# Edge loads at a round's second landing, x1 stored without a hold at B's end, five z rounds fetched there

## The chip, the cores and the metric

The kernel runs on one core of a Trainium2 chip. The metric is the device time of one execution in microseconds; lower is better. All tensors are fp32.

## The reference

Two layers of a graph network over 50000 nodes of 128 features, with 25000 edges sorted by target `dst`:

```python
h = relu(layernorm(x))
agg = segment_sum(h[src], dst) / max(deg, 1)            # layer 0: mean over a node's edges
x = x + agg @ W_l.T + h @ W_r.T                         # x1
h = relu(layernorm(x))
agg = segment_sum(edge_attr, src)                       # layer 1: sums by source
h = bn(silu(concat(h, agg) @ W1 + b1))                  # batch norm over all 50000 nodes
h = bn(silu(h @ W2 + b2))
x = x + h @ W3 + b3
```

## The kernel before

The nodes are cut into 49 rounds (the last is short); a round has 1024 nodes (8 chunks of 128) and 512 edges (4 chunks of 128). Rounds go in pairs: `i` counts pairs, `par` is 0 or 1, r = 2i + par, `RF` = 48 is the tail and `IT` = 24. There are five phases, one behind the other in each engine's program.

- **A** gathers x by `src`, normalises, multiplies by W_l and scatters with accumulation into `acc1` (L916); it stores y = x + h @ W_r.T.
- **B** makes x1 = acc1 / deg + y, stores it, and multiplies relu(layernorm(x1)) with the upper half of W1 (this is z, kept in `zT` or, for every third round, spilled to `z_dram`). Beside it B sums the edge rows of equal source within 512 edges, multiplies them with the lower half of W1 and scatters them into `acc2` (L936).
- **C** loads `acc2`, transposes it on PE (L1748), adds it to z (L1518), takes silu and its statistics. **F** multiplies by w2 (L1777) and **G** by w3 (L1787), with the x1 that B stored.

**B's scatter** (`scatter_b`, POOL) has four indirect DMAs a round, one for each chunk of 128 edges. Their landings count on three semaphores: chunks 0 and 1 on `s_sc2`, chunk 2 on `s_mid2`, chunk 3 on `s_end2`. Chunk 0 of a round waits for the landing of chunks 0 and 1 of the round before, chunk 1 for that of chunk 2, chunk 2 for that of chunk 3. ACT copies the rows for the scatter into a ring of four tiles (`vrow_b`, in `zT` and `tabs`), L1028.

**SP's queue in B** is written out round by round in `step_b`, called by `written_out` with the rounds r - 1, r, r + 1, r + 2 and r + 3 (`before`, `now`, `after`, `ahead`, `third`). For round r, in this order: at the second landing (`s_sc2`) it loads y of round r + 3 if that is a spilled round; at `s_mid2`, with the sums made (`B["added"]`), it stores x1 of round r into `x1_dram` (named `x_dram` in the profile's tiles); at `s_end2` it loads the nodes of round r + 3 (512 KB of `acc1`, L581) and with `load_b_edges` the edges of round r + 4: `halves` (2 KB, the sources' names as two fp16 rows, L667) and `rows` (256 KB of edge attributes, L669). `rows` is one tile for each `par`, so the load first waits for PE's sums of round r + 2 (`B["summed"]`, `presum`, L1646). `halves` feeds PE's `spread_names_b` (L1691), whose product DVE compares with the names of the edges' columns (`match`, L1290). The sums of x1 are DVE's L1456.

In step r, PE sums edges of round r + 2 and spreads names of round r + 3; DVE adds the nodes of round r and compares the names of round r + 2; ACT copies the scattered rows of round r + 2.

**The turn from B to C.** Rounds 32 to 48 of z were spilled. Ten of them are fetched back into `zT` (`fetch`, 512 KB each, L686). Seven are fetched early, at B's end: five before round 47's x1 store, when PE's last edge product is done (`v_ready`), into the place of B's edge tiles, and two before round 48's store, into the place of `aux`, when the sums are made. Three follow between C's loads. Before C's first load SP waits for all scatters, for all four x1 slots' stores and for ACT's normalised rows. C's loads go into `res` and `xin` in turn, which are the four slots of x1 (rounds 46 and 47 in `res`, 48 and 45 in `xin`).

Of the kernel before, what the change touches and what calls it, by code (L numbers as in the profile page):

```python
# [11 lines left out]
ROUND = 2 * GROUP  # L12


def this(sem, par, i, inc=1):

    return sem[par], (i + 1) * inc


def two_ago(sem, par, i, inc=1):  # L20

    return sem[par], i * inc
# [12 lines left out]
def gnn_layers(nc, x, src, dst, edge_attr, WlT, WrT, W1, b1, g1, be1, W2, b2, g2, be2, W3, b3, out):  # L35
# [27 lines left out]
    RF = N // ROUND  # L63
    IT = RF // 2
# [5 lines left out]
    KEPT = 16  # L70
# [8 lines left out]
    MID_C = 11  # L79
# [7 lines left out]
    assert FETCHED == 10  # L87
    EARLY_FETCHED = 7
    ACC_ROWS = 3 * P * -(-(N + GROUP) // (3 * P))
# [7 lines left out]
    RING = 4  # L97
# [35 lines left out]
    with ctx:  # L133
# [62 lines left out]
        sumT = part([P, ROWS, P])  # L196
        assert taken[0] == (2 * KEPT + EARLY_FETCHED - 2) * ROUND
        aux = part([P, 2, CHUNKS, D])
# [371 lines left out]
        def _(sp):  # L570
# [87 lines left out]

            def load_b_edges(i, par, tail, spill, held=False):

                r = 2 * i + par
                p = EDGE_TAIL if tail else P
                if type(i) is not int or i:
                    sp.wait_ge(*spread(par, i - 1))
                if held:
                    sp.wait_ge(*two_ago(s_end2, par, i - 1, 16))
                sp.dma_start(halves[:, par, :], src_halves[r]).then_inc(B["row_loaded"][par], 16)  # L667
                sp.wait_ge(*two_ago(B["summed"], par, i))
                sp.dma_start(rows[0:p, par, :, :].rearrange("p j d -> p (j d)"), ea_v[1] if tail else ea_v[0][r])\  # L669
                    .then_inc(B["rows_loaded"][par], 16)  # L670
# [13 lines left out]
            def fetch(k):  # L684

                sp.dma_start(zT[:, 2 * KEPT + k, :], z_dram[k]).then_inc(s_fetched, 16)  # L686

            def fetch_early(r):

                if r == RF - 1:  # L690
                    for par in range(2):
                        sp.wait_ge(B["z_stored"][par], 16 * 4)
                        sp.wait_ge(*this(B["v_ready"], par, IT - par))
                    for k in range(EARLY_FETCHED - 2):
                        fetch(k)
                if r == RF:
                    sp.wait_ge(*this(B["added"], 0, IT))
                    sp.wait_ge(*this(B["added"], 1, IT - 1))
                    for k in range(EARLY_FETCHED - 2, EARLY_FETCHED):
                        fetch(k)  # L700

            def step_b(before, now, after, ahead, third):

                i, par, tail, spill, slot, node = now
                fetch_early(2 * i + par)
                sp.wait_ge(*this(s_sc2, par, i, 32))
                if not before and ahead:
                    load_b_nodes(*ahead)
                if third and third[3]:
                    if before:  # L710
                        sp.wait_ge(*this(B["act_normed"], *before[1::-1]))
                    load_b_y(*third)
                sp.wait_ge(*this(s_mid2, par, i, 16))
                sp.wait_ge(*this(B["added"], par, i))
                store_nodes(x1_ring[slot], x1_v, 2 * node[0] + node[1], tail, x1_stored[slot], HALF_RUN)
                if third:
                    sp.wait_ge(*this(s_end2, par, i, 16))
                    load_b_nodes(*third)
                if type(i) is not int or 2 * (i + 2) + par <= RF:
                    load_b_edges(i + 2, par, type(i) is int and i + 2 == IT, 0, held=True)  # L720


# [14 lines left out]
            sp.wait_ge(*this(s_end2, 1, IT - 1, 16))  # L737
            for k in range(RING):
                r = RF - (RF - k) % RING
                sp.wait_ge(x1_stored[k], x1_count(r // 2, k, r == RF))  # L740
            sp.wait_ge(*this(B["act_normed"], 0, IT))
# [25 lines left out]
            def store_z(ph, d, n, i, par, tail=False, place=z_later):  # L767
                sp.wait_ge(*this(ph["silu"], par, n))
                sp.wait_ge(*this(ph["stats"], par, n))
                for a, b in spilled(d[2 * (i - KEPT_LATER) + par], place(i, par), tail):  # L770
                    sp.dma_start(a, b).then_inc(ph["stored"][par], 16)

            def pre_activations(i, par, tail=False):
                load_late(z_dram, KEPT, i, par, tail, z_later(i, par))

            for n in range(2):
                for par in range(2):
                    load_c(n, n, n, par)
            reload_fixed(2, 3)
# [5 lines left out]
            for par in range(2):  # L785
                store_z(C, zz_dram, 3, IT - 1, par)
            reload_loop(7, 9, 1)
            for par in range(2):
                sp.wait_ge(C["stored"][par], 16)
                pre_activations(KEPT_LATER, par)  # L790
            sp.wait_ge(s_fetched, 16 * EARLY_FETCHED)
            fetch(7)
            reload_loop(9, MID_C, 1)
            reload_fixed(MID_C, MID_C + 1)
            sp.wait_ge(s_fetched, 16 * 8)
            fetch(8)
            reload_fixed(MID_C + 1, MID_C + 2)
            reload_loop(MID_C + 2, MID_C + 4, 2)
            sp.wait_ge(s_fetched, 16 * 9)
            fetch(9)  # L800
            reload_loop(MID_C + 4, KEPT + 1, 2)
# [1022 lines left out]
```

## Time and profile before

| | us |
|---|---|
| median of 3 runs | 1402.36 (1400.37 to 1403.76) |
| profiled execution | 1403.72, its span 1402.0 |
| A's scatters and gathers | about 90 to 625 |
| B | about 625 to 1062 |
| C | 1065.8 (first load) to 1179 |
| F | 1179.5 to 1266 |
| G | to the end |

| engine | busy us | share of the span |
|---|---|---|
| DVE | 1072.2 | 76% |
| PE | 1014.0 | 72% |
| POOL | 879.6 | 63% |
| ACT | 876.0 | 62% |

A busy share is a mean over phases with different limits. The time between two landings, and what a transfer waits for, stand in the timelines and in the chain of work that ended last. POOL's busy time is that of issuing an indirect DMA (some 1.5 us each); the DMA itself lands later.

### The profile page before, as it was taken

Reading aid. Unit: us, or ns where it says so; the run is one execution under the profiler, and the core shown is the slowest. Engines: PE = TensorE matmul, PEld = TensorE weight load, DVE = VectorE, ACT = ScalarE, POOL = GpSimd, SP = SyncE. Lnnn points to the kernel's source line nnn. Section 1 sums busy time; section 2 is a strip of 40 time slices with the busy share of each in tenths; the row PEclk is TensorE's granted clock in tenths of the full one; section 3 lists DMA queues with packets and bytes.
Section 4 is the critical chain, followed back from the end, with each engine's and each line's share of the span. In section 5 each row is a group of like instructions: output and inputs, shape, how many; then the busy total and the mean of one; then the engine's idle time right before and its main releaser. Section 6 shows DMA issues by size and latency. Waiting matters only on the chain.

```text
span 1402.0 us, 22062 instructions
## 1 busy us (share of the span) xinstructions
PE 1014.0 (72%) x5275; PEld 732.3 (52%) x5275; DVE 1072.2 (76%) x4647; ACT 876.0 (62%) x1708; POOL 879.6 (63%) x625
## 2 busy tenths in 40 slices
PE   0227677677776666766988888898976667999776
PEld 0125555555554444544655656565654553447765
DVE  2428888888877667666999899998963887788966
ACT  1227677677765565552877777786874876669610
POOL 7778788888888888876777777877761000002443
PEclk9969999999999998897999999998987878999999
DMA  9988888877776666667899999999989983216999
GB/s 331 371 298 198 221 209 211 215 171 159 172 159 137 139 154 136 135 146 185 204 240 234 239 233 223 263 220 240 228 241 289 352 276 122 90 60 237 418 418 362
DMA packets 184284, 313.25 MB, mean 223 GB/s; under 512 B 21840, under 2 KB 73462, under 8 KB 184194
## 3 DMA queue, kind: packets, MB, share of 16 engines
q1 hardware_dynamic: 116026, 264.44, 54.3%
q0 software_dynamic: 62720, 38.57, 23.2%
q10 hardware_dynamic: 5448, 9.29, 1.8%
q8 instruction: 26, 0.43, 0.1%
q14 instruction: 64, 0.52, 0.1%
HBM read 162.44 MB, written 149.79 MB: 223 GB/s over the span
## 4 chain that ended last, share of the span: by engine, by line
POOL 43%; DMA 22%; issue 17%; PE 11%; DVE 4%; ACT 1%; SPq 0%; DVEq 0%; POOLq 0%; ACTq 0%
POOL acc L916 22%; POOL acc L936 10%; DMA acc<-zT,worn 8%; POOL xin L894 7%; PE ps L1777 6%; DMA acc<-tabs,worn 5%; POOL zT L902 4%; DMA zT<-x_dram 4%; PE ps L1748 2%; DMA xin<-acc 2%; DMA res<-acc 1%; PE ps L1787 1%; DMA acc<-zT,tabs 1%; DVE zT L1598 1%; DVE zT L1602 1%
## 5 line engine op out<-in xcount | busy, mean ns | idle before, releaser
L1646 PE MATMUL ps<-zT 128*128 128x512 f32 (+5 forms) x784 | 272.7, 499 | 135.5 <-ACT zT L1055 128.0
L916 POOL DMA_INDIRECT acc<-zT,tabs x196 | 317.4, 1619 | 68.4 <-issue 62.0
L1646 PEld LDWEIGHTS ps<-zT 128*128 128x128 f32 (+1 forms) x784 | 165.3, 217 | 264.3 <-issue 134.9
L1381 DVE BATCH_NORM_STATS2 zT<-zT 128x6 f32<-128x128 f32 (+1 forms) x384 | 78.9, 278 | 170.8 <-DMA zT<-in_x_dram 170.8
L936 POOL DMA_INDIRECT acc<-zT,worn x100 | 156.6, 1566 | 53.5 <-issue 26.2
L936 POOL DMA_INDIRECT acc<-tabs,worn x96 | 150.2, 1565 | 52.2 <-issue 25.1
L894 POOL DMA_INDIRECT xin<-in_x_dram,tabs x140 | 141.3, 1009 | 42.6 <-issue 42.1
L1015 ACT ACTIVATE hT<-ps 128x1024 f32<-128x1024 f32 (+1 forms) x100 | 100.1, 1003 | 65.7 <-PE ps L1638 53.1
L1656 PE MATMUL ps<-weights_ab,zT 128*128 128x128 f32 (+1 forms) x784 | 126.4, 286 | 5.7 <-ACT zT L1022 5.3
L1638 PE MATMUL ps<-ident,zT 128*128 128x128 f32 (+1 forms) x784 | 118.9, 301 | 8.2 <-ACT zT L1007 7.6
L1290 DVE SCALAR_TENSOR_TENSOR zT<-ps,worn,zT 128x128 f32<-128x128 f32 (+1 forms) x196 | 95.2, 541 | 37.4 <-PE ps L1691 37.1
L1679 PE MATMUL ps<-weights_ab,hT 128*128 128x128 f32 (+1 forms) x784 | 100.8, 284 | 30.6 <-DVE zT L1372 30.4
L1679 PEld LDWEIGHTS ps<-weights_ab,hT 128*128 128x128 f32 (+1 forms) x784 | 96.9, 198 | 38.2 <-issue 35.6
L1007 ACT ACTIVATE zT<-zT 128x128 f32<-128x128 f32 (+1 forms) x288 | 115.3, 479 | 0.0
L1656 PEld LDWEIGHTS ps<-weights_ab,zT 128*128 128x128 f32 (+1 forms) x784 | 107.3, 199 | 11.9 <-ACT zT L1022 11.5
L973 POOL TENSOR_TENSOR zT<-zT,b3b 128x1024 f32 (+1 forms) x21 | 49.6, 2364 | 100.5 <-DMA zT<-x_dram 100.5
L1787 PE MATMUL ps<-w,zT 128*128 128x128 f32 x768 | 93.1, 278 | 26.6 <-DVE zT L1602 24.7
L1638 PEld LDWEIGHTS ps<-ident,zT 128*128 128x128 f32 (+1 forms) x784 | 99.1, 157 | 24.1 <-ACT zT L1007 12.4
L1787 PEld LDWEIGHTS ps<-w,zT 128*128 128x128 f32 x768 | 88.1, 192 | 32.2 <-issue 26.2
L1022 ACT ACTIVATE zT<-ps 128x512 f32<-128x512 f32 (+1 forms) x98 | 57.8, 590 | 72.3 <-PE ps L1646 65.5
L1722 PE MATMUL ps<-hT,weights_ab 128*128 128x512 f32 (+1 forms) x196 | 98.1, 626 | 3.6 <-ACT hT L1015 3.6
L1507 DVE BATCH_NORM_STATS2 bst<-zT (+1 forms) x126 | 80.6, 684 | 25.6 <-ACT zT L1168 20.1
(194 smaller groups left out, 2145.9 us busy)
## 6 DMA issues: line engine op xcount, KB each, us to landing
acc<-bst SPq DMA_DIRECT2D x12, 2112.0 KB, 20.4
acc<-bst SPq DMA_DIRECT2D x48, 528.0 KB
zT<-in_x_dram SPq DMA_DIRECT2D x48, 512.0 KB, 6.5
zT<-acc SPq DMA_DIRECT2D x48, 512.0 KB, 4.8
zT<-x_dram SPq DMA_DIRECT2D x42, 512.0 KB, 10.0
out_dram<-zT SPq DMA_DIRECT2D x42, 512.0 KB, 10.2
zT<-row_dram SPq DMA_DIRECT2D x49, 256.0 KB, 5.7
zT<-in_edge_attr_dram SPq DMA_DIRECT2D x48, 256.0 KB
```

Of the source, the lines that this page charges most:

```text
L894: pool.indirect_dma_start(row_ring[:, k % RING, j, :], None, x, bass.IndirectOffsetOnAxis(ap=icol[:, c:c + 1], axis=0)).then_inc(s_ring[k ...
L916: pool.indirect_dma_start(acc1, bass.IndirectOffsetOnAxis(ap=target_a[:, k, j:j + 1], axis=0), v[:, j, :], None, compute_op=ALU.add).then_ ...
L936: pool.indirect_dma_start(acc2, bass.IndirectOffsetOnAxis(ap=target_b[:, k, j:j + 1], axis=0), vrow_b[k % RING][:, j, :], None, compute_op ...
L1007: ins = nc.scalar.activation(to[0:p, c, :], t[0:p, c, :], ACT.Identity, bias=nm[0:p, par, k:k + 1], scale=rs[0:p, par, k:k + 1])
L1015: ins = nc.scalar.activation(hT[:, par, c, 0:p], psR[:, c, 0:p], ACT.Relu)
L1290: ins = nc.vector.scalar_tensor_tensor(same[0:p, par, at:at + j + 1, 0:p], row[0:p, 0:j + 1, 0:p], columns_of(ph, i, par)[0:p, 0, j:j + 1] ...
L1638: ins = nc.tensor.transpose(ps_t[:, c, 0:p], t[0:p, c, :], ident[0:p, 0:p])
L1646: ins = nc.tensor.matmul(psA[:, 0:j + 1, 0:p], t[0:p, j, :], same[0:p, par, at:at + j + 1, 0:p], start=(j == ROWS - 1), stop=(j == 0))
L1656: ins = nc.tensor.matmul(psV[0:p, j, :], sumT[:, j, 0:p], w[:, :], start=True, stop=not taken_over)
L1679: ins = nc.tensor.matmul(psQ[0:q, c, :], hT[:, par, c, 0:q], wr[:, :], start=True, stop=True)
L1722: ins = nc.tensor.matmul(psQ[:, c, 0:q], w1a[:, :], hT[:, par, c, 0:q], start=True, stop=True)
L1787: ins = nc.tensor.matmul(ps2[par][0:q, c, :], g_place(i, par)[:, c, 0:q], w3[:, :], start=True, stop=True)
```

## The change

`load_b_edges` is called right after the wait for the second landing (`s_sc2`) of round r, ahead of y's load, and no longer waits for `s_end2`. Rounds 47 and 48 (no `third`) store x1 without waiting for any landing. `EARLY_FETCHED` is 5: the five fetches stand at the head of round 48's step (behind round 47's store), the two others move into C, where now five fetches are spread over the loads, each waiting for the one before. The wait for all four x1 stores ahead of C is gone; each of C's first four loads waits for the store of its own slot.

```diff
--- before.py
+++ after.py
@@ -85,7 +85,7 @@
                                           for i in range(SPILLED, 2 * SPILLED))
     FETCHED = 2 * (KEPT_LATER - KEPT)
     assert FETCHED == 10
-    EARLY_FETCHED = 7
+    EARLY_FETCHED = 5
     ACC_ROWS = 3 * P * -(-(N + GROUP) // (3 * P))
     ZPARTS = 12
     ZREP = 2
@@ -194,7 +194,7 @@
         irow = part([P, 2, ROWS, P])
         rows = part([P, 2, ROWS, D])
         sumT = part([P, ROWS, P])
-        assert taken[0] == (2 * KEPT + EARLY_FETCHED - 2) * ROUND
+        assert taken[0] == (2 * KEPT + EARLY_FETCHED) * ROUND
         aux = part([P, 2, CHUNKS, D])
         hE = part([P, 2, ROWS, D])
         order = part([P, ROWS, P])
@@ -656,14 +656,12 @@
                 x1_slot_free(sp, i, slot)
                 load_nodes(x1_ring[slot], y_v, 2 * node[0] + node[1], tail, B["y_loaded"][par], HALF_RUN)
 
-            def load_b_edges(i, par, tail, spill, held=False):
+            def load_b_edges(i, par, tail, spill):
 
                 r = 2 * i + par
                 p = EDGE_TAIL if tail else P
                 if type(i) is not int or i:
                     sp.wait_ge(*spread(par, i - 1))
-                if held:
-                    sp.wait_ge(*two_ago(s_end2, par, i - 1, 16))
                 sp.dma_start(halves[:, par, :], src_halves[r]).then_inc(B["row_loaded"][par], 16)
                 sp.wait_ge(*two_ago(B["summed"], par, i))
                 sp.dma_start(rows[0:p, par, :, :].rearrange("p j d -> p (j d)"), ea_v[1] if tail else ea_v[0][r])\
@@ -685,40 +683,36 @@
 
                 sp.dma_start(zT[:, 2 * KEPT + k, :], z_dram[k]).then_inc(s_fetched, 16)
 
-            def fetch_early(r):
-
-                if r == RF - 1:
-                    for par in range(2):
-                        sp.wait_ge(B["z_stored"][par], 16 * 4)
-                        sp.wait_ge(*this(B["v_ready"], par, IT - par))
-                    for k in range(EARLY_FETCHED - 2):
-                        fetch(k)
-                if r == RF:
-                    sp.wait_ge(*this(B["added"], 0, IT))
-                    sp.wait_ge(*this(B["added"], 1, IT - 1))
-                    for k in range(EARLY_FETCHED - 2, EARLY_FETCHED):
-                        fetch(k)
+            def fetch_early():
+
+                for par in range(2):
+                    sp.wait_ge(B["z_stored"][par], 16 * 4)
+                    sp.wait_ge(*this(B["v_ready"], par, IT - par))
+                for k in range(EARLY_FETCHED):
+                    fetch(k)
 
             def step_b(before, now, after, ahead, third):
 
                 i, par, tail, spill, slot, node = now
-                fetch_early(2 * i + par)
-                sp.wait_ge(*this(s_sc2, par, i, 32))
+                if tail:
+                    fetch_early()
+                if third:
+                    sp.wait_ge(*this(s_sc2, par, i, 32))
                 if not before and ahead:
                     load_b_nodes(*ahead)
+                if 2 * (i + 2) + par <= RF:
+                    load_b_edges(i + 2, par, i + 2 == IT, 0)
                 if third and third[3]:
                     if before:
                         sp.wait_ge(*this(B["act_normed"], *before[1::-1]))
                     load_b_y(*third)
-                sp.wait_ge(*this(s_mid2, par, i, 16))
+                if third:
+                    sp.wait_ge(*this(s_mid2, par, i, 16))
                 sp.wait_ge(*this(B["added"], par, i))
                 store_nodes(x1_ring[slot], x1_v, 2 * node[0] + node[1], tail, x1_stored[slot], HALF_RUN)
                 if third:
                     sp.wait_ge(*this(s_end2, par, i, 16))
                     load_b_nodes(*third)
-                if type(i) is not int or 2 * (i + 2) + par <= RF:
-                    load_b_edges(i + 2, par, type(i) is int and i + 2 == IT, 0, held=True)
-
 
             sp.wait_ge(*this(s_sc1, 0, IT, 64))
             sp.wait_ge(*this(s_sc1, 1, IT - 1, 64))
@@ -735,9 +729,6 @@
             sp.wait_ge(*this(s_mid2, 1, IT - 1, 16))
             sp.wait_ge(*this(s_end2, 0, IT, 16))
             sp.wait_ge(*this(s_end2, 1, IT - 1, 16))
-            for k in range(RING):
-                r = RF - (RF - k) % RING
-                sp.wait_ge(x1_stored[k], x1_count(r // 2, k, r == RF))
             sp.wait_ge(*this(B["act_normed"], 0, IT))
             sp.wait_ge(*this(B["act_normed"], 1, IT - 1))
 
@@ -770,11 +761,18 @@
                 for a, b in spilled(d[2 * (i - KEPT_LATER) + par], place(i, par), tail):
                     sp.dma_start(a, b).then_inc(ph["stored"][par], 16)
 
+            def fetch_next(k):
+                sp.wait_ge(s_fetched, 16 * k)
+                fetch(k)
+
             def pre_activations(i, par, tail=False):
                 load_late(z_dram, KEPT, i, par, tail, z_later(i, par))
 
             for n in range(2):
                 for par in range(2):
+                    k = par if n else 2 + par
+                    r = RF - (RF - k) % RING
+                    sp.wait_ge(x1_stored[k], x1_count(r // 2, k, r == RF))
                     load_c(n, n, n, par)
             reload_fixed(2, 3)
             all_stored(B["z_stored"], KEPT)
@@ -784,20 +782,18 @@
             reload_loop(5, 7, 1)
             for par in range(2):
                 store_z(C, zz_dram, 3, IT - 1, par)
+            fetch_next(5)
             reload_loop(7, 9, 1)
             for par in range(2):
                 sp.wait_ge(C["stored"][par], 16)
                 pre_activations(KEPT_LATER, par)
-            sp.wait_ge(s_fetched, 16 * EARLY_FETCHED)
-            fetch(7)
+            fetch_next(6)
             reload_loop(9, MID_C, 1)
-            reload_fixed(MID_C, MID_C + 1)
-            sp.wait_ge(s_fetched, 16 * 8)
-            fetch(8)
-            reload_fixed(MID_C + 1, MID_C + 2)
+            fetch_next(7)
+            reload_fixed(MID_C, MID_C + 2)
+            fetch_next(8)
             reload_loop(MID_C + 2, MID_C + 4, 2)
-            sp.wait_ge(s_fetched, 16 * 9)
-            fetch(9)
+            fetch_next(9)
             reload_loop(MID_C + 4, KEPT + 1, 2)
             reload_fixed(KEPT + 1, KEPT + 2)
             pre_activations(IT, 0, True)
```

## Rows read from the trace of the kernel before

**Rows 1.** the page, part 4: engines' shares of the chain that ended last
```profile
POOL 43%; DMA 22%; issue 17%; PE 11%; DVE 4%; ACT 1%; SPq 0%; DVEq 0%; POOLq 0%; ACTq 0%
```

**Rows 2.** windows of B's middle and C: busy us (x), clock, DMA share, GB/s
```profile
680.00:1049.00 369.00, 322.67 (x1557) 220.23 (x1555) 333.41 (x1870) 284.73 (x584) 277.52 (x178) 0.96 0.93 233
...
1066.00:1157.00 91.00, 54.81 (x336) 49.12 (x336) 74.14 (x88) 67.27 (x98) 0.00 (x0) 0.79 0.90 316
```

**Rows 3.** waits of DVE and PE, 680 to 1000: us, times, longest
```profile
DVE zT L1290 <- PE ps L1691: 20.4, 15, 2.4
...
PE ps L1691 <- DMA zT<-half_dram: 30.9, 21, 3.1
```

**Rows 4.** waits of POOL, 680 to 1000
```profile
POOL acc L936 <- DMA acc<-zT,worn: 23.1, 17, 3.0
...
POOL acc L936 <- DMA acc<-tabs,worn: 12.3, 11, 2.2
```

**Rows 5.** timeline of POOL: start, us, operation, [idle before <- releaser]
```profile
682.51 1.70 POOL L936 DMA_INDIRECT acc<-zT,worn  x1 [0.46 <-issue]
...
791.62 1.54 POOL L936 DMA_INDIRECT acc<-zT,worn  x1 [0.99 <-DMA acc<-zT,worn]
...
824.02 1.54 POOL L936 DMA_INDIRECT acc<-zT,worn  x1 [0.40 <-issue]
...
831.65 1.54 POOL L936 DMA_INDIRECT acc<-tabs,worn  x1 [0.30 <-issue]
...
833.50 1.55 POOL L936 DMA_INDIRECT acc<-tabs,worn  x1 [0.30 <-issue]
...
840.80 1.54 POOL L936 DMA_INDIRECT acc<-tabs,worn  x1 [2.02 <-DMA acc<-tabs,worn]
...
1049.27 1.54 POOL L936 DMA_INDIRECT acc<-zT,worn  x1 [1.48 <-DMA acc<-tabs,worn]
...
1055.98 1.55 POOL L936 DMA_INDIRECT acc<-zT,worn  x1 [0.30 <-issue]
```

**Rows 6.** the scatter's line L936, 680 to 1000
```profile
DMA to landing us min/median/max: 3.3/5.0/7.1
```

**Rows 7.** timeline of SP's issues in round 22
```profile
833.04 0.38 SPq L588 DMA_DIRECT2D x_dram<-xin  x1
...
834.61 0.38 SPq L581 DMA_DIRECT2D zT<-acc  x1
...
835.43 0.36 SPq L669 DMA_DIRECT2D zT<-in_edge_attr_dram  x1
```

**Rows 8.** DMA view, 830 to 862: slices of 0.8 us; KB, us to landing
```profile
GB/s 358 362 370 344 88 250 401 141 296 284 348 163 88 19 0 335 305 169 326 313 302 130 28 75 215 263 384 378 251 342 265 293 330 369 179 25 380 282 58 150
...
zT<-acc SPq DMA_DIRECT2D x4, 512.0 KB, 4.7
```

**Rows 9.** DMA view, 680 to 1000: SP's queue, packets, MB, share
```profile
q1 hardware_dynamic: 30063, 57.15, 53.8%
```

**Rows 10.** timeline of PE, the edge sums of round 18
```profile
790.21 2.32 PE L1646 MATMUL ps<-zT 128*128 128x512 f32 x8
```

**Rows 11.** timeline of DVE, the sums of round 24
```profile
842.57 2.24 DVE L1456 SCALAR_TENSOR_TENSOR xin<-zT,worn 128x128 f32<-128x128 f32 x8
```

**Rows 12.** chain that ended last, 1000 to 1180: start, us, what
```profile
1054.14 8.04 DMA acc<-zT,worn
...
1062.61 2.85 DMA x_dram<-xin
...
1065.84 3.51 DMA res<-acc
```

**Rows 13.** timeline of SP's issues at B's end
```profile
1043.04 2.47 SPq L686 DMA_DIRECT2D zT<-z_dram  x5
...
1052.55 1.30 SPq L686 DMA_DIRECT2D zT<-z_dram  x2
```

**Rows 14.** the same chain in C
```profile
1092.08 5.95 DMA xin<-acc
```

## What the change is predicted to do

> **What bounds the kernel now.** I read the page's chain that ended last first: POOL, the engine that issues the gathers and scatters, has 43% of it and DMA 22% [rows 1]. The edit lies in B, in the turn from B to C and in C, so I went on with the windows of those stretches. In B's middle no engine is idle for long (DVE 333.4 of 369 us, DMA engines 0.93), and C's first 91 us have the DMA engines at 0.90 and 316 GB/s [rows 2]. Shares don't say what ends last, so the next view is who waited for whom in 680 to 1000. DVE's waits there are 20.4 us on the name product of L1691, and PE's are 30.9 us on the halves load that this product reads [rows 3]. They look like what the change removes. But POOL's waits in the same 320 us are 35.4 us, all for its own earlier scatters (28 times); it never waits for a row that ACT has yet to copy [rows 4]. So B's pace is a loop of POOL with DMA: chunk 0 of a round waits until chunks 0 and 1 of the round before have landed. DVE's 20 us are the slack of an engine that is ahead.
>
> POOL's timeline gives the size. Chunk 0 starts at 682.51 in round 4 and at 1049.27 in round 48, so a round takes 366.76 / 44 = 8.34 us. Four issues of 1.55 and four gaps of 0.30 are 7.42, so 0.92 us a round, 40 us in all, is waiting for landings [rows 5]. One round shows how: chunk 1, issued at 833.50, landed some 6.5 us later, since the next chunk 0 went at 840.80 after 2.02 us of idleness [rows 5]. The least that a scatter took from issue to landing is 3.3, the median 5.0, the most 7.1 [rows 6]. Meanwhile SP had issued the x1 store at 833.04, the 512 KB node load at 834.61 and the 256 KB edge load at 835.43 [rows 7], and the DMA engines moved 280 to 350 GB/s until about 839; then three slices of 0.8 us have 88, 19 and 0 GB/s, and the same burst begins anew [rows 8]. A burst at the end of a round lengthens the scatter's landing, and a hole stands after it.
>
> **The change, part by part.** (1) *Edge loads go from the last to the second landing.* Nothing is added or removed, 2 DMAs a round (2 KB and 256 KB) move ahead of the y load, the x1 store and the node load in SP's queue. DVE's and PE's waits of [rows 3] vanish (the halves land earlier), and I cost that at nothing: POOL doesn't wait for it. SP's queue moves 57.15 MB in 53.8% of 320 us [rows 9], 332 GB/s, so an edge load is 262 KB / 332 = 0.79 us of the DMA engines. It leaves the end of a burst, where chunk 1 is still in flight, and enters the hole behind the second landing. In the two rounds of three without a y load I take half of it as an earlier landing of chunk 1, 0.40 us. In the third round y is issued at that landing already, there is no hole, so 0. The mean is 0.26. Against it, the chunks 2 and 3 that are in flight at the second landing share the engines with the edges: 0.10, an estimate of an eighth of 0.79. Net 0.16 x 44 = **-7.0 us**. Bounds: 0.40 in every round is -17.6; the loss is that of the third rival, +11.
>
> New waits in part 1: SP now asks at the second landing whether PE has summed the edges of round r+2, whose tile the load overwrites. Queued behind it are y, x1's store and the nodes of round r+3. In most rounds the sum is done; at its latest PE ended it at 792.53 [rows 10] with the next chunk 0 at 791.62 [rows 5], so SP would stand for about 1.7 us. Who waits for that? The nodes: issued at 834.61 [rows 7], their adds begin at 842.57 [rows 11], and such a load takes 4.7 [rows 8], so 3.2 us cover it. I cost it at 0; without that cover it would be 1.7 us in perhaps one round of five (an estimate from that row), 44 / 5 x 1.7 = 15 us for DVE, of which POOL, which has copied rows in stock, would feel a part. The same answers the two `wait_ge` that go for rounds 47 and 48: no load follows them.
>
> (2) *x1 stored without a hold, C's loads by their buffers.* Before, the tail's x1 store is issued only when the last scatters have landed, is waited for (1062.61, 2.85 us), and the first load of C goes at 1065.84, 3.65 us after the last scatter's landing at 1062.18 [rows 12]. After, it is stored when its sums are made, right behind the five fetches of 1043 [rows 13], and the first loads (tiles `res`) ask for the stores of rounds 46 and 47, done long before. Some waits remain (0.03 each): **-3.3 us**; bounds -3.6 and, if PE's filler products (L1756) end late, -2.
>
> (3) *Five rounds fetched instead of seven at B's end.* The two 512 KB loads at 1052.55 [rows 13] go, which stood right ahead of the scatter that took 8.04 us [rows 12]. The five stay at 1043.04, because PE's last product of edges sets them before and after. The last chunk, issued at 1055.98 [rows 5], then lands after about the median 5.0 [rows 6] at 1061.0 instead of 1062.2: **-1.2**; bounds 0 and -2.9 (3.3 us to landing). The two come back in C: 524 KB / 316 GB/s [rows 2] = 1.66 us each, ahead of a reload that stands on the chain (1092.08, 5.95 us [rows 14]) and of another some 25 us later. The engines are at 0.90 there, so I take nine tenths: **+3.0**; bounds 0 and +3.3. `fetch_next`'s waits are for fetches issued 10 us or more before: 0.
>
> Sum: -7.0 - 3.3 - 1.2 + 3.0 = -8.5. The profiled execution took 1403.7 (span 1402.0), so 1395.2; the median of the runs, 1402.4, is 1.4 lower, so **1394** (1393.9).
>
> **The rivals.** *First, the end only.* The scatter's landing may not feel the edges: their packets stand behind the nodes', and chunk 1 may be through before them. Then the 0.92 us a round stay and the sum is -1.5: 1401 (1398 to 1403). For it: landings differ between 3.3 and 7.1 in rounds with equal loads. Against it: the hole after the burst. The Trainium skill, DMA: Bandwidth & Descriptors, Queues, rings and completion order, says that each DMA engine goes round between the queues that have work, packet by packet. By that rule a deep SP queue costs a scatter only its turn; the sum would be this rival's -1.5. The trace bears it out in part: scatters do land while the burst runs, though late. The same time comes out if the edges don't in fact go earlier, because SP stands on PE's sum.
>
> *Second, the whole gain.* If the burst's end sets each landing of chunk 1, 0.40 a round comes through: -17.6 - 1.5 = -19.1, 1383. Against it: a round such as that from 824.02 to 831.65, 7.63 us [rows 5], has little to give, and once chunk 0 doesn't wait, chunk 1 waits for chunk 2 (chunk 1 can wait for chunk 2 of the round before instead).
>
> *Third, slower.* The edges now run at the moment at which chunks 2 and 3 are in flight and chunk 0 of the next round is issued, and in the y rounds they stand in front of an already closed row of y, x1 and nodes: 1.8 MB with no hole. If chunk 0 and 1 then land 0.25 us later on the mean (0.75 in every third round, nearly the 0.79 of the edge load), 0.25 x 44 = 11.0, less 1.5: +9.5, 1412. It decides for slower as soon as the added landing time passes 1.5 / 44 = 0.03 us plus 0.06 (2.8 us, what can be told from no change), about 0.1 us a round. For it: every scatter in flight at that landing is one that POOL waits for a round later; against it: the holes of [rows 8].
>
> **How the numbers follow.** Forecast 0.40 (1388 to 1399); the end only 0.30 (1398 to 1403); the whole gain 0.08; slower 0.22 (1403.5 to 1412, most below 1408). Within 0.2% is 1399.6 to 1405.2, about what a measurement of this kernel can tell from no change. Faster: 0.40 + 0.08 + a third of 0.30 = 0.58. Same: 0.20 and 0.04 of the slower ones = 0.24. Slower: 0.18. The range leaves out half of the whole gain below and about 0.14 of the slower above: 1384 to 1405.
>
> **What would show it.** In the profile after: POOL's chunk 0 of rounds 4 and 48 some 360 us apart instead of 366.8 (step 1; at 366 the first rival, at 370 or more the third); DVE's wait for L1691 near zero with no such gain, which would show it as slack; no rise of SP's waits for L1646 above some 10 us; the first load of C within 0.5 us of the last scatter's landing (step 2); that landing some 5 us after its issue (step 3); C's stretch from its first load to F's first product 2 to 3 us longer. It would be wrong if the waits of POOL move from one chunk to another with the sum unchanged, or if C loses more than B's end gives.

## The result, and the profile after

The changed kernel takes 1423.7 us (median of 6 runs, 1421.8 to 1429.4), the kernel before 1401.4 (6 runs). The ratio is 1.0175, with a 95% interval of 1.0151 to 1.0199: slower by 1.75%, some 22 to 25 us. Forecast were 1394 and a range of 1384 to 1405. The change did what it says, and what was costed as a gain of 7 us in B turned into a loss of some 28.

The windows of B's middle and of C's first 91 us (us; busy time and count of PE, PEld, DVE, ACT, POOL; clock, DMA share, GB/s) answer to [rows 2]; the first line is the kernel before in the same 320 us as the second, which is the kernel after. In these 320 us POOL now issues 144 scatters, before it was 156 (36 rounds for 39), and the DMA engines are *less* busy, 0.85 for 0.93. C is as fast as before:

```profile
680.00:1000.00 320.00, 284.85 (x1376) 194.24 (x1375) 295.14 (x1653) 248.71 (x510) 242.97 (x156) 0.96 0.93 233
680.00:1000.00 320.00, 269.87 (x1286) 182.76 (x1286) 275.03 (x1540) 232.59 (x474) 222.81 (x144) 0.96 0.85 217
1088.00:1179.00 91.00, 57.06 (x351) 50.58 (x350) 74.45 (x88) 67.81 (x99) 0.00 (x0) 0.84 0.93 337
```

Who waited for whom, 680 to 1000, POOL, then DVE, then PE (total us, times, longest). POOL's waits for its scatters were 35.4 us in 28 waits [rows 4]; now they are 60.4 in 29. DVE's 20.4 us on the name product [rows 3] are gone, and in their place stand 43.5 us on the loads of nodes, which never kept it waiting before. PE's wait for the halves, 30.9 us before, is still there:

```profile
POOL acc L932 <- DMA acc<-zT,worn: 31.4, 15, 4.3
POOL acc L932 <- DMA acc<-tabs,worn: 29.0, 14, 3.5
...
DVE res L1452 <- DMA zT<-acc: 26.2, 16, 4.3
DVE xin L1452 <- DMA zT<-acc: 17.3, 13, 3.3
...
PE ps L1687 <- DMA zT<-half_dram: 31.9, 23, 3.1
```

The scatter line, same stretch. The least and the median are within 0.1 us of those of [rows 6] (3.3 and 5.0), but the longest landing went from 7.1 to 8.8:

```profile
DMA to landing us min/median/max: 3.2/4.9/8.8
```

POOL's timeline: chunk 0 of round 4, the four chunks of round 21, chunk 0 of round 22 and chunk 0 of round 48. From round 4 to 48 it is 1078.25 - 679.20 = 399.05 us, 9.07 a round, for 8.34 before [rows 5]:

```profile
679.20 1.54 POOL L932 DMA_INDIRECT acc<-zT,worn  x1 [1.83 <-DMA acc<-tabs,worn]
...
831.66 1.68 POOL L932 DMA_INDIRECT acc<-zT,worn  x1 [1.05 <-DMA acc<-zT,worn]
833.64 1.56 POOL L932 DMA_INDIRECT acc<-zT,worn  x1 [0.30 <-issue]
835.50 1.54 POOL L932 DMA_INDIRECT acc<-zT,worn  x1 [0.30 <-issue]
837.35 1.55 POOL L932 DMA_INDIRECT acc<-zT,worn  x1 [0.30 <-issue]
841.67 1.54 POOL L932 DMA_INDIRECT acc<-tabs,worn  x1 [2.77 <-DMA acc<-zT,worn]
...
1078.25 1.54 POOL L932 DMA_INDIRECT acc<-zT,worn  x1 [3.31 <-DMA acc<-tabs,worn]
```

And SP's issues in that same stretch, with ACT's store of z. This is the picture of the loss:

```profile
830.88 0.26 SPq L665 DMA_DIRECT2D zT<-half_dram  x1
831.19 0.36 SPq L667 DMA_DIRECT2D zT<-in_edge_attr_dram  x1
831.64 0.39 SPq L581 DMA_DIRECT2D res<-y_dram  x1
832.12 0.42 SPq L588 DMA_DIRECT2D x_dram<-xin  x1
832.64 0.42 SPq L581 DMA_DIRECT2D zT<-acc  x1
840.90 0.26 SPq L665 DMA_DIRECT2D zT<-half_dram  x1
841.21 0.36 SPq L667 DMA_DIRECT2D zT<-in_edge_attr_dram  x1
841.69 0.38 SPq L588 DMA_DIRECT2D x_dram<-xin  x1
842.18 0.41 SPq L581 DMA_DIRECT2D zT<-acc  x1
```
```profile
833.81 0.33 ACTq L1100 DMA_DIRECT2D z_dram<-hT  x1
```

Within 1.8 us of the second landing SP has issued edges, y, x1 and nodes, 1.8 MB, and 1.2 us later ACT adds z, 2.4 MB in all. The chunks issued at 831.66 to 837.35 are behind it: SP's next issue at a second landing is at 840.90, and x1 and nodes follow without a pause, since chunks 2 and 3 have landed too. Before, the same kind of round (its chunk 0 at 848.74) had its transfers in three groups, and z at 854.19, 5.5 us into the round, not 2.2:

```profile
847.95 0.38 SPq L581 DMA_DIRECT2D res<-y_dram  x1
848.42 0.72 SPq L588 DMA_DIRECT2D x_dram<-res  x1
851.04 0.38 SPq L581 DMA_DIRECT2D zT<-acc  x1
851.51 0.30 SPq L667 DMA_DIRECT2D zT<-half_dram  x1
851.86 0.36 SPq L669 DMA_DIRECT2D zT<-in_edge_attr_dram  x1
```
```profile
854.19 0.33 ACTq L1104 DMA_DIRECT2D z_dram<-hT  x1
```

The chain at the turn to C (start, us, what) answers to [rows 12]. The last chunk lands 4.70 us after its issue and C's first load follows 0.25 us behind. No x1 store stands between:

```profile
1083.80 4.70 DMA acc<-zT,worn
...
1088.75 3.73 DMA res<-acc
```

The account of the two profiled executions (span 1402.0 and 1421.8), by chunk 0 of rounds 4, 44 and 48, C's first load and the statistics' end in C and F (us; worked out from the timelines):

| stretch | before | after | difference |
|---|---|---|---|
| start to round 4 | 682.5 | 679.2 | -3.3 |
| rounds 4 to 44 | 331.1 | 359.4 | +28.3 |
| rounds 44 to 48 | 35.6 | 39.7 | +4.1 |
| round 48 to C's first load | 16.6 | 10.5 | -6.1 |
| C from its first load | 112.1 | 110.4 | -1.7 |
| F and G | 224.0 | 222.6 | -1.4 |

A "y round" is one that begins, with its chunk 0, when y is loaded; it is every third. Nearly the whole loss sits there: the 13 y rounds among rounds 4 to 43 went from 8.37 to 10.42 us (26.7 us together), the 27 others from 8.23 to 8.29 (1.6 us).

### The profile page after: what moved, and what is told of

Read it like the earlier page. It is cut to its first block, busy times and chain, and to the rows that moved or that the text cites. A ratio compares the mean times of both kernels' runs of the same rounds, so it can differ in the third digit from the quotient of the medians.

```text
span 1421.8 us, 22055 instructions
## 1 busy us (share of the span) xinstructions
PE 1010.7 (71%) x5275; PEld 730.9 (51%) x5275; DVE 1060.2 (75%) x4647; ACT 877.7 (62%) x1708; POOL 877.5 (62%) x625
## 4 chain that ended last, share of the span: by engine, by line
POOL 40%; DMA 28%; issue 16%; PE 10%; DVE 3%; ACT 1%; SPq 1%; POOLq 0%; DVEq 0%; ACTq 0%
POOL acc L912 20%; DMA acc<-zT,worn 9%; POOL acc L932 9%; DMA acc<-tabs,worn 8%; POOL xin L890 7%; DMA zT<-x_dram 7%; PE ps L1773 6%; POOL zT L898 4%; DMA xin<-acc 3%; PE ps L1744 1%; DVE zT L1514 1%; ACT zT L1137 1%; DMA acc<-zT,tabs 1%; DVE bst L1503 1%; PE ps L1642 1%
## 5 line engine op out<-in xcount | busy, mean ns | idle before, releaser
L1642 PE MATMUL ps<-zT 128*128 128x512 f32 (+5 forms) x784 | 258.1, 477 | 140.3 <-ACT zT L1051 131.6
L1642 PEld LDWEIGHTS ps<-zT 128*128 128x128 f32 (+1 forms) x784 | 156.6, 207 | 265.2 <-issue 134.5
L1652 PE MATMUL ps<-weights_ab,zT 128*128 128x128 f32 (+1 forms) x784 | 129.8, 291 | 16.0 <-ACT zT L1018 15.9
L1675 PEld LDWEIGHTS ps<-weights_ab,hT 128*128 128x128 f32 (+1 forms) x784 | 100.2, 203 | 41.5 <-issue 39.0
L1634 PEld LDWEIGHTS ps<-ident,zT 128*128 128x128 f32 (+1 forms) x784 | 95.4, 154 | 37.2 <-ACT zT L1003 28.0
L1783 PE MATMUL ps<-w,zT 128*128 128x128 f32 x768 | 96.4, 281 | 22.8 <-DVE zT L1598 21.7
L996 ACT ACTIVATE zT<-zT,eps 128x12 f32<-128x12 f32 x98 | 29.5, 301 | 116.9 <-DVE zT L1397 107.6
```

Of the source, the lines that this page charges most:

```text
L1634: ins = nc.tensor.transpose(ps_t[:, c, 0:p], t[0:p, c, :], ident[0:p, 0:p])
L1642: ins = nc.tensor.matmul(psA[:, 0:j + 1, 0:p], t[0:p, j, :], same[0:p, par, at:at + j + 1, 0:p], start=(j == ROWS - 1), stop=(j == 0))
L1652: ins = nc.tensor.matmul(psV[0:p, j, :], sumT[:, j, 0:p], w[:, :], start=True, stop=not taken_over)
L1675: ins = nc.tensor.matmul(psQ[0:q, c, :], hT[:, par, c, 0:q], wr[:, :], start=True, stop=True)
L1783: ins = nc.tensor.matmul(ps2[par][0:q, c, :], g_place(i, par)[:, c, 0:q], w3[:, :], start=True, stop=True)
```

## The experiments

All figures in one table first. Each ratio is to executions of the kernel before that were taken together with that run (medians 1400.2 to 1403.6), so medians of different rows compare less well than ratios. "Round" is the mean from chunk 0 of round 4 to that of round 44, "y round" the mean of the 13 y rounds, "nodes" and "z" are the mean times at which the node load and z's store of the y round leave, counted from its chunk 0 (all from the timelines of POOL, SP and ACT; one profile a kernel). "Held" is z issued at the next second landing. One of c1's ten executions took 2439.16 us; its ratio leaves that one out.

| kernel | median | ratio (95%) | round | y round | nodes | z |
|---|---|---|---|---|---|---|
| before | 1401.4 | 1 | 8.28 | 8.37 | +2.4 | +6.5 |
| after | 1423.7 | 1.0175 (1.0151 to 1.0199) | 8.98 | 10.42 | +1.1 | +2.3 |
| a1 edges early only | 1429.3 | 1.0188 (1.0139 to 1.0238) | 8.90 | 10.38 | +1.3 | +2.5 |
| a2 end only | 1398.5 | 0.9963 (0.9937 to 0.9988) | 8.31 | 8.38 | +2.5 | +6.3 |
| a3 edges late in y steps | 1407.8 | 1.0044 (1.0017 to 1.0070) | 8.44 | 8.87 | +2.0 | +5.0 |
| a4 halves early only | 1411.9 | 1.0081 (1.0051 to 1.0110) | 8.61 | 9.20 | +2.3 | +3.7 |
| a5 rows early only | 1403.1 | 1.0013 (0.9992 to 1.0035) | 8.56 | 9.24 | +1.7 | +6.2 |
| b1 after, z held | 1414.2 | 1.0077 (1.0048 to 1.0106) | 8.63 | 9.27 | +1.1 | held |
| b2 a4, z held | 1399.9 | 0.9998 (0.9972 to 1.0023) | 8.47 | 8.76 | +2.3 | held |
| b3 a2, z held | 1397.9 | 0.9967 (0.9944 to 0.9991) | 8.35 | 8.62 | +2.1 | held |
| c1 a3, z held | 1406.2 | 1.0032 (1.0006 to 1.0058) | 8.45 | 8.69 | +1.7 | held |
| c2 a2, y last | 1403.6 | 1.0006 (0.9980 to 1.0032) | 8.45 | 9.42 | +1.5 | +6.3 |
| c3 b1, rows cut | 1390.3 | 0.9917 (0.9890 to 0.9945) | 8.07 | 8.43 | +2.5 | held |
| c4 b3, rows cut | 1380.6 | 0.9856 (0.9820 to 0.9892) | 7.93 | 7.84 | +3.1 | held |
| d1 after, nodes wait | 1414.3 | 1.0117 (1.0082 to 1.0152) | 8.60 | 9.37 | +3.4 | +3.8 |
| d2 b1, nodes wait | 1392.5 | 0.9938 (0.9919 to 0.9957) | 8.29 | 8.87 | +3.2 | held |
| d3 a2, seven fetched | 1393.1 | 0.9950 (0.9922 to 0.9978) | 8.31 | 8.55 | +2.1 | +6.1 |
| d4 a2, nodes wait for x1 | 1386.6 | 0.9911 (0.9887 to 0.9935) | 7.99 | 8.30 | +6.1 | +9.6 |
| e1 b1, nodes wait for x1 | 1409.4 | 1.0046 (1.0022 to 1.0070) | 8.51 | 8.72 | +6.9 | held |
| e2 b3, nodes wait for x1 | 1389.1 | 0.9898 (0.9869 to 0.9927) | 8.04 | 8.35 | +6.3 | held |

### Which part of the change it is

a1 is the kernel before with this alone:

```diff
+                if 2 * (i + 2) + par <= RF:
+                    load_b_edges(i + 2, par, i + 2 == IT, 0)
                 if third and third[3]:
...
-                if type(i) is not int or 2 * (i + 2) + par <= RF:
-                    load_b_edges(i + 2, par, type(i) is int and i + 2 == IT, 0, held=True)
```

> The kernel before with the edge loads at the second landing and nothing else. Theory A (the edge loads bunch SP's transfers in front of the scatters): B takes all of the loss and the gain of the end is missing, so some 29 us over before less the 3 us by which A ended earlier in the profile: 1421 to 1431, a round of B 9.0 us. Rival E (the end of B costs it): 1393 to 1401, a round 8.3 us.

Measured 1429.3, ratio 1.0188, 8.90 a round. a2 is the changed kernel with the two lines of `load_b_edges` put behind `load_b_nodes(*third)`:

> The changed kernel with the edge loads back behind the node load, so only x1's stores, the fetches and C's loads differ from before. Theory A: the first load of C 3.4 us nearer to the last landing and C no longer than before: 1393 to 1398, a round of B 8.3 us. Rival E: 1415 or more.

Measured 1398.5, ratio 0.9963. So the end's edits are worth 0.37% (5 us), and the edge loads at the second landing cost 1.0175 - 0.9963 = 2.1%, 30 us (a1 alone says 1.9%, 26 us). The rest of the study is about these 30.

### Four loads in a row, or the compute that runs ahead

a3 keeps the early edges out of the steps in which y is loaded:

```diff
-                if 2 * (i + 2) + par <= RF:
+                early = not (third and third[3])
+                if early and 2 * (i + 2) + par <= RF:
                     load_b_edges(i + 2, par, i + 2 == IT, 0)
...
                     load_b_nodes(*third)
+                if not early and 2 * (i + 2) + par <= RF:
+                    load_b_edges(i + 2, par, i + 2 == IT, 0)
```

> The changed kernel, but in every third step, in which y is loaded too, the edges stay behind the node load. Theory A in its narrow form (four loads in a row in the y step do the harm): the rounds of 10.4 us fall to some 8.4, a round 8.3 us on the mean, 1393 to 1400. Rival W (each early edge load costs its share): a third of the loss goes, 1410 to 1416.

Measured 1.0044: the y rounds fall to 8.87, most of the loss goes, yet 0.8% (11 us) over a2 stays, with early edges in the two other steps alone. Neither expectation fits. z leaves at +5.0 here, 1.3 us earlier than in a2. a4 splits `load_b_edges` and moves only the 2 KB of `halves`, `rows` (256 KB) stays last; a5 is the reverse:

> The changed kernel, but only the 2 KB halves load goes at the second landing; the 256 KB rows load stays behind the node load. Theory A (traffic of the rows load): as without the edit, a round of B 8.3 us, 1393 to 1398, while DVE no longer waits for L1687. Rival D (what harms is that PE and DVE run ahead once the halves come early, so that the node load and the z stores fall elsewhere): 1415 to 1425.

> The changed kernel, but only the 256 KB rows load goes at the second landing, the 2 KB halves load stays behind the node load and so still holds back PE's name product. The theory now, Z: the early halves let DVE and ACT run 2 us ahead, so ACT's 512 KB store of z, which left at +5.6 us of a y round before, leaves at +2.3 us, into y, x1 and the nodes. Z: z at +5 or later, y rounds near 8.5 us, a round 8.3 to 8.4, 1396 to 1404. Rival A (the rows' traffic in the y round): y rounds 9.5 or more, 1410 to 1420.

a4 was the surprise: 1.0081, 1.2% (17 us) over a2, for moving 2 KB, between its two expectations. The rows (a5), 128 times the bytes, cost 0.5% (7 us): the time is what theory Z expected, but the y rounds are not (9.24 us, with z as late as in a2), so early rows slow the y rounds with z in its place. The two together cost more than their sum (2.1% for 1.7%). In a4 z leaves at +3.7 us of a y round, in a2 at +6.3 (the expectations have +3.4 and +5.6, which miss the latest stores). DVE's waits, 680 to 1000, in a2 and then in a4, say why: with late halves it stands on the name product, with early halves it runs on until the nodes aren't there.

```profile
DVE zT L1286 <- PE ps L1687: 23.0, 19, 2.9
```
```profile
DVE res L1460 <- DMA zT<-acc: 14.9, 8, 3.2
DVE zT L1294 <- PE ps L1695: 8.6, 5, 2.8
DVE xin L1460 <- DMA zT<-acc: 8.4, 5, 3.7
```

That made a theory that can be tried without touching SP's queue: hold z's store alone.

```diff
                     act.wait_ge(*this(B["z_copied"], par, i))
+                    if 2 * i + par < RF - 1:
+                        act.wait_ge(*this(s_sc2, 1 - par, i + par, 32))
                     for d, t in spilled(z_dram[...], hT[:, par, :, :], tail):
```

> The changed kernel, with one wait more: ACT issues the store of a spilled round's z only at the second landing of the next round's scatter, some 7 us into the y round, for rounds below 47. Theory Z alone: the y rounds fall from 10.4 to about 8.6, 1396 to 1403. Rival A alone: they stay at 10 or more, 1420 or more. Both in part: 1405 to 1415.

> As b1, on the kernel with the halves load alone at the second landing (9.20 us in y rounds, z at +3.4). Z: y rounds 8.4, mean round 8.3, within 3 us of the kernel with the end's edit alone (1398). Rival D (running ahead harms in another way, by where the node loads fall): 8.6 on the mean, 1408 or more.

> The control: the same wait on the kernel with the end's edit alone, where z left at +5.6 already. It shows what the wait itself costs: if ACT's standing still some 2 us in every third round is free, 1396 to 1401, a round 8.3; if it isn't, b1 and b2 have to be read against this one.

The control b3 is 0.9967 beside a2's 0.9963: the wait is free. With it a4 falls from 1.0081 to 0.9998 (12 of its 17 us), the changed kernel from 1.0175 to 1.0077 (14 of 30). So the early z store is shown as half of the loss, and as most of what the halves do (b2 is still 0.3%, 4 us, over the control). b1 is still 1.1%, 15 us, over its control.

### What the other half is

c1 is a3 with the same hold:

> The changed kernel with edges early only in the two steps without a y load, and z's store held until the second landing. Z and the y round's queue together are then undone. If those two are all of the loss: 1395 to 1401, a ratio within 0.2% of the control b3 (0.9967), y rounds at 8.5. If early edges cost in the other rounds as well: 1402 or more.

1.0032, 0.65% over the control: early edges in the two other steps cost as well. The narrow form (four loads in a row in one step of three) falls. c2 asks whether a load at the second landing is bad as such, and moves y behind the nodes and edges in a2:

> The kernel with the end's edit alone (0.9963), and the y load moved from the second landing to behind the node and edge loads. Theory Q (what SP issues at the second landing stands in front of the next chunks 0 and 1, what it issues behind the nodes falls in their slack): chunk 0 of the y round lands 0.7 us sooner, y rounds below 8.1, 1386 to 1394. Rival (the same bytes in a round cost the same wherever they stand, and y now meets z): 1396 to 1404.

1.0006, 0.4% over a2 (their intervals overlap by 0.0008). The rounds between became shorter, 7.98 us for 8.27 in a2, but the y rounds, in which y now leaves at +2.8, took 9.42: what is taken from the front isn't free at the back, where it meets z and the chunks that follow. c3 and c4 cut the bytes of the rows load from round 4 on; their edge sums read stale rows, so their output is not the reference's:

```diff
+                q = ROWS * D if i < 2 else 32
-                sp.dma_start(rows[0:p, par, :, :].rearrange("p j d -> p (j d)"), ea_v[1] if tail else ea_v[0][r])\
-                    .then_inc(B["rows_loaded"][par], 16)
+                sp.dma_start(rows[0:p, par, :, :].rearrange("p j d -> p (j d)")[:, 0:q],
+                             (ea_v[1] if tail else ea_v[0][r])[:, 0:q]).then_inc(B["rows_loaded"][par], 16)
```

> b1 (both early, z held) with the rows load cut from 2048 to 128 bytes a partition from round 4 on, so its edge sums are of stale rows and the output isn't the reference's. With the next one it separates the bytes of the rows load from its place in the order. Bytes: the distance to the next one falls from 1.1% to that of the halves alone, 0.3% (4 us). Order (the wait for PE's sums in front of y, x1 and nodes, or the issue itself): it stays near 1.1%, 15 us.

> b3 (end's edit, edges late, z held) with the same cut rows load, also not the reference's output. If the rows' bytes at the end of the burst lengthen the landing of chunks 0 and 1, as the forecast has it (0.26 us a round), 11 us below b3, 1387; if they stand in slack there, within 4 us of b3, 1394 to 1399.

Late, the bytes cost 0.9967 - 0.9856 = 1.1% (16 us, 0.35 a round); early, 1.0077 - 0.9917 = 1.6% (22 us). So they cost in either place, some 7 us more in front. The distance between early and late falls from 15 us to 0.6% (8.5 us), half way between the two answers. Some of the loss is bytes in front of the chunks and some is order. How much of each stays open: with the bytes gone, c3's nodes leave at +2.5, in b1 at +1.1, so bytes and distance changed together.

The table shows the order in the column "nodes". In the kernel before the node load, which waits for chunk 3, left at +2.4. With edges first, x1 and nodes leave right behind them, the nodes at +1.1. In the rounds that come just before a y round, chunk 3 landed 4.7 us after its issue before and 3.4 after (means of 13, from the landings of its semaphore); chunk 2 did not land sooner (3.8 and 4.1). The hold in d1 and d2 makes a distance by another event. It is wider than that of before: in d2 the nodes leave at +3.2 in the y rounds and in the others too, where before they left at +1.5:

```diff
                     sp.wait_ge(*this(s_end2, par, i, 16))
+                    if 2 * (i + 2) + par <= RF:
+                        sp.wait_ge(B["rows_loaded"][par], 16 * (i + 3))
                     load_b_nodes(*third)
```

> The changed kernel, with the node load of each step held until the rows load issued at the same step has landed, so that nodes leave at +2.5 us or later of a round instead of +0.6 to +1.1. Theory S (the loss that is left is that x1 and nodes leave together and sit in front of chunks 0 and 1): the round falls from 8.98 to 8.6 to 8.7, 1408 to 1415, and DVE and z come later too. Rival P (place of the edge bytes in front of the chunks is enough by itself): no change or worse, 1420 or more.

> The same hold of the node load with z's store held too (b1: ratio 1.0077, 8.63 a round). S: 8.35 to 8.45 a round, ratio 0.997 to 1.001. P: 1.005 or more.

d1 gains 0.6% (8 us) on the changed kernel, with z still early at +3.8. d2 gains 1.4% (19 us) on b1 and ends at 0.9938, with the edges still loaded at the second landing: not above the 0.9967 of the control, and below what was expected of it. POOL's waits for its scatters, 680 to 1000, are back at 36.7 us, for 60.4 in the changed kernel and 50.7 in b1:

```profile
POOL acc L934 <- DMA acc<-zT,worn: 18.6, 12, 2.6
POOL acc L934 <- DMA acc<-tabs,worn: 18.1, 13, 3.7
```

In the sum nothing of the 30 us is left, but that is not yet a proof that z's place and the nodes' distance were all of it. d2's y rounds still take 8.87 us, in the control 8.62; its other rounds take 8.02, in the control 8.22, so the hold gains there what is still lost in the y rounds. And a hold of the node load gains where the edges are late as well (0.5% and 0.7% in the next section). z's place is shown as half of the loss; for the other half the distance of the nodes is the likely cause in part, and its share is not isolated.

### Further apart, and a version that beats both

If distance is what helps, the order of before should gain too. d4 is a2 with one wait:

```diff
                     sp.wait_ge(*this(s_end2, par, i, 16))
+                    sp.wait_ge(x1_stored[slot], x1_count(i, slot, tail))
                     load_b_nodes(*third)
```

> The kernel with the end's edit alone (0.9963), with each step's node load held until that step's x1 store has landed, so that nodes leave at +3 to +4 us instead of +1.2 to +2.5. S in its strong form (further apart is better): 4 to 10 us faster than the kernel with the end's edit alone, 1388 to 1394. If the stagger is at its best there or the loads then come late for DVE: 1398 or more.

0.9911 (0.9887 to 0.9935): 1386.6 us, 0.5% below a2, faster than the kernel before and the changed one. A round takes 7.99, the nodes leave at +6.1 of a y round (the expectation had +3 to +4), and POOL's waits for its scatters are down to 29.1 us in 680 to 1000:

```profile
POOL acc L933 <- DMA acc<-tabs,worn: 16.6, 19, 2.0
POOL acc L933 <- DMA acc<-zT,worn: 12.5, 16, 2.4
```

The landings' least, median and most in the same stretch are 3.2, 5.0 and 6.4; the changed kernel's most was 8.8:

```profile
DMA to landing us min/median/max: 3.2/5.0/6.4
```

The longest landing alone doesn't tell the pace: b1's is 6.2, and POOL waits 50.7 us there. Whether d4 gains by the distance between the transfers or by the later start of the node load as such isn't told apart.

The last pair puts d4's wait on both places of the edges, z held in both:

> The changed kernel (edges at the second landing), z's store held, and the node load held until the step's x1 store has landed. If z's place and the lost stagger are all of the loss, the early edges now lie in the hole as the forecast had it: as fast as e2 or up to 7 us faster, 1380 to 1388. If their bytes in front of chunks 0 and 1 cost by themselves: 4 us or more slower than e2.

> The same with the edge loads behind the node load. It differs from d4 by z's hold alone, whose price was within the noise in b3: 1384 to 1391, a ratio near 0.991.

e2 is 0.9898 (1389.1), 0.7% below its own control b3; e1 is 1.0046 (1409.4): 1.5% apart. The first expectation of e1 failed, but not as a proof that bytes in front are dear. SP's timeline in e1 and then in e2 shows that the wait regrouped the queue. It made SP late for the next second landing, so in e1 nodes, edges and x1 leave together, and x1, whose landing the next node load waits for, is the last of 1.3 MB; in e2 x1 goes 2.9 us behind nodes and edges:

```profile
830.34 0.38 SPq L581 DMA_DIRECT2D zT<-acc  x1
830.81 0.28 SPq L665 DMA_DIRECT2D zT<-half_dram  x1
831.14 0.36 SPq L667 DMA_DIRECT2D zT<-in_edge_attr_dram  x1
831.62 0.83 SPq L588 DMA_DIRECT2D x_dram<-xin  x1
838.86 0.38 SPq L581 DMA_DIRECT2D zT<-acc  x1
```
```profile
832.86 0.38 SPq L581 DMA_DIRECT2D zT<-acc  x1
833.29 0.33 SPq L665 DMA_DIRECT2D zT<-half_dram  x1
833.67 0.36 SPq L667 DMA_DIRECT2D zT<-in_edge_attr_dram  x1
836.60 0.38 SPq L588 DMA_DIRECT2D x_dram<-res  x1
839.86 0.38 SPq L581 DMA_DIRECT2D zT<-acc  x1
```

So e1 doesn't tell whether early edges would cost if all else stayed apart. The nearest pair is d2 and e2, both with z and the node load held, though by different events: 0.9938 (0.9919 to 0.9957) with early edges, 0.9898 (0.9869 to 0.9927) with late ones, 0.4% or 6 us apart with intervals that overlap. Early edges may still cost that much.

### The fetches

d3 is a2 with seven fetched at B's end, the last two right behind round 48's x1 store.

> The kernel with the end's edit alone (0.9963), but seven rounds fetched at B's end as before: two of them right behind round 48's x1 store at about 1046, not at 1052. The forecast's terms (1.2 lost at the last landing, 3.0 saved in C): 2 us faster than it, 1396 if it is at 1398. If the two fetches in C are free: 0 to 3 us slower.

0.9950 (0.9922 to 0.9978) beside 0.9963 (0.9937 to 0.9988): the intervals overlap. The forecast's 2 us fit, and so does no difference. From its first load, C takes 107.3 us in d3's profile and 109.8 in a2's, but the profiles of the other kernels with five early fetches lie between 108.6 and 113.8; this term stays open.

## Why the prediction was wrong, point by point

**The bound was read rightly.** POOL with its own landings sets B's pace before and after: its waits grew from 35.4 / 39 = 0.91 to 60.4 / 36 = 1.68 us a round, by 0.77, and the round by 0.73. Two of the statements around it failed.

**"DVE's and PE's waits of [rows 3] vanish (the halves land earlier), and I cost that at nothing: POOL doesn't wait for it."** This is the step that failed first. DVE's did vanish; PE's did not (31.9 us for 30.9), it only waits at an earlier time of the round (the product starts 0.9 us into the y round of 831.66, before 6.6 us into that of 848.74). POOL didn't wait for DVE in either kernel. But DVE's wait was what kept DVE and ACT back, and ACT's queue holds a 512 KB store every third round. It moved from +6.5 to +2.3 us of the y round, right behind y, x1 and nodes, and b1 and b2 price that at 14 and 12 us. The question "what does the released engine start earlier, and what does it collide with" wasn't asked. I followed SP's queue and not ACT's.

**"Net 0.16 x 44 = -7.0 us", the hole behind the landing.** Its bytes were sized about rightly: by c4 the rows load at the back costs 0.35 us a round, and 0.26 were taken. Wrong was that the rest stays in its place. I let chunks 2 and 3 land 0.10 *later*. In rounds without y chunk 3 landed sooner, 3.4 us after its issue for 4.1, and chunk 2 0.2 sooner (4.1 for 4.2); in y rounds both landed later (6.4 for 5.3 and 5.0 for 4.7), yet before or together with the next chunk 0 and not 0.7 and 2.0 us behind it. Either way x1 and nodes left closer to the second landing, and chunks 0 and 1, which were to gain 0.26 us a round, landed 9.63 us after the issue of chunk 0 in y rounds, for 7.45 before. d1 and d2 show that holding the nodes back gets much of this again; that early edges are then free is not shown. The row of [rows 8] was also read too smoothly: besides the hole behind the burst it has 88 and 141 GB/s within it.

**The third rival** had the sign and the place: chunks 0 and 1 land later in y rounds. Its mechanism, the edge load's 0.79 us in front of them, is the smaller part (the bytes cost 22 us early by c3 and 16 late by c4, so 7 for their place). It gave 11 us where 30 were measured; z's move, some 14 of them, and the nodes' weren't in it. Its limit, 0.1 us a round, was passed sevenfold: +0.73. It had 0.22, and the range ended at 1405.

**The first rival and the page's rule.** The Trainium skill (DMA: Bandwidth & Descriptors, Queues, rings and completion order) has each DMA engine go round between queues with work. Here four chunks issued over 5.7 us (831.66 to 837.35) landed within 1.5 us (840.1 to 841.6) behind a burst on two other queues; the first took 8.5 us. Of all between 680 and 1000 the longest took 8.8 and the shortest 3.2, where the last large load had been issued 4.7 us earlier. So no run here bears out that a scatter pays its turn only; the landings were later where more had been issued on the other queues. Which resource is behind that, these runs don't show.

**SP's new wait for PE's sums** was costed at 0, and is: 1.1 us in 680 to 1000.

**The end.** Forecast -3.3 (no hold) and -1.2 (last chunk), together 4.5; measured from round 48's chunk 0 to C's first load 16.6 to 10.5, -6.1. What I left out is that rounds 44 to 48 lengthen by 4.0 in a2 as well, where the stores of x1 of rounds 46 and 47 and five fetches follow each other; they lengthen by 3.1 in a1 too, whose end is that of before, so the cause is not shown. C was to lose 3.0 to the two fetches and is 1.7 (changed kernel) and 2.3 us (a2) shorter in the profiles. No run shows that term as a loss; whether it was hidden by something else d3 can't decide. The sum of the end was -1.5, a2 shows -5 (0.37%).

## What to carry to other kernels

A wait that no critical engine waits for can still be a pacing wait: before it is costed at nothing, list what the engines behind it issue, DMAs above all, and where in the period these will fall. Where scatters or other short DMAs are bound by landing, look at the distance between the large transfers as well as at their sum (c4 shows that the sum counts too); a load that waits on another one's landing (d4) bought 0.5% with no byte less. And an order of loads in which each is released by a landing feeds back on itself: moving one of them moves all that are released after it.

## What the runs showed of the hardware

- A scatter of 128 rows (four of them a round) lands 3.2 us after its issue at best, in the changed kernel as in d4, and up to 8.8 us where 2.4 MB were issued on the two other queues within 3 us around it. The four chunks of such a round land almost together (840.1 to 841.6 above).
- 2 KB loaded 2.4 to 4 us earlier cost 17 us over the kernel (a4 beside a2), of which 12 went when z was held (b2), while taking 240 KB a round away gained 16 (c4).
- DMA engines at 0.93 of their time gave more rounds in 320 us (39) than at 0.85 (36): the lower share was that of bunching, with holes between, as the kernel after shows from 831 on, in slices of 0.8 us (holes from about 841, 847 and 856):

```profile
GB/s 71 62 271 192 271 399 399 397 369 372 319 180 59 8 131 376 397 328 309 207 88 70 9 80 97 341 407 244 303 263 141 65 10 97 12 6 46 61 384 417
```
